# Patch embedding of a small vision tower: token rows 1 and 2 share one product with summed weights, rows in the order 0, 3, 1, 2

## The reference

```python
p = PATCH                                   # 16
shifts = ((1, -1, 1, -1), (-1, 1, -1, 1), (-1, 1, 1, -1), (1, -1, -1, 1))
parts = [x] + [_shift2d(x, HALF * s[2], HALF * s[0]) for s in shifts]
xc = jnp.concatenate(parts, axis=1)         # image and four copies shifted by 8
patches = ...reshape(B, h * w, p * p * C5)  # 16 tokens of 3840 values
mu = patches.mean(axis=-1, keepdims=True)
var = patches.var(axis=-1, keepdims=True)
xn = (patches - mu) * jax.lax.rsqrt(var + LN_EPS) * ln_gamma + ln_beta
return jnp.einsum('bnp,dp->bnd', xn, W) + b # 192 values a token
```

## Time and profile before

| what | us |
|---|---|
| median of 3 runs | 692.64 |
| the profiled execution, its own time | 691.0 |
| its span, first to last instruction | 689.2 |
| PE busy (share of the span) | 506.5 (73%) |
| DVE busy | 354.6 (51%) |
| ACT busy | 163.7 (24%) |
| POOL busy | 156.5 (23%) |
| L680, the patch products: busy | 99.1 |
| first product of `qk(0)` at | 122.4 |

### The profile page before, as it was taken

How to read it: one execution, slowest core, us unless ns; L and a number is a source line. 1 busy time by engine, 2 the same in 40 slices (tenths; PEclk the granted TensorE clock), 3 DMA queues, 4 the chain that set the end, 5 groups by cost and what they waited for, 6 DMA issues and landing times.

```text
span 689.2 us, 13111 instructions
## 1 busy us (share of the span) xinstructions
PE 506.5 (73%) x4632; PEld 450.1 (65%) x4633; DVE 354.6 (51%) x1088; ACT 163.7 (24%) x341; POOL 156.5 (23%) x156
## 2 busy tenths in 40 slices
PE   4999996996314516199999269621899999999960
PEld 4999996456313413189998266401799999999960
DVE  1599995466999885522212567667122212222216
ACT  4100001223793224043332040300221222112210
POOL 2894000000001000224442100001244444444320
PEclk9999998998656558599999789865799999999995
DMA  9960000000004002376659500202666555655516
GB/s 327 412 220 11 1 1 0 2 3 2 1 0 162 1 0 92 81 206 178 176 161 351 179 1 0 92 0 64 186 175 178 174 164 172 179 173 160 139 48 249
DMA packets 35235, 81.41 MB, mean 118 GB/s; under 512 B 6870, under 2 KB 17970, under 8 KB 34034
## 3 DMA queue, kind: packets, MB, share of 16 engines
q1 hardware_dynamic: 29618, 69.36, 30.8%
q0 software_dynamic: 5568, 11.41, 6.3%
HBM read 70.33 MB, written 10.42 MB: 117 GB/s over the span
## 4 chain that ended last, share of the span: by engine, by line
PE 63%; DVE 23%; DMA 5%; ACT 4%; issue 3%; SPq 1%; POOL 0%; ACTq 0%; DVEq 0%; POOLq 0%
PE ps L925 17%; PE ps L680 13%; PE ps L905 11%; PE ps L909 7%; DMA xT<-rows,from_i 2%; DVE stat L1028 2%; PE ps L750 2%; PE ps L751 2%; DVE h L1574 2%; PE ps L778 1%; PE ps L864 1%; DMA arena<-tok_w 1%; DVE xT L1450 1%; PE ps L890 1%; PE ps L655 1%
## 5 line engine op out<-in xcount | busy, mean ns | idle before, releaser
L925 PE MATMUL ps<-arena,xn 128*128 x696 | 128.1, 334 | 0.6 <-ACT xn L596 0.6
L925 PEld LDWEIGHTS ps<-arena,xn 128*128 128x128 f32 x696 | 111.5, 190 | 7.5 <-issue 0.8
L680 PE MATMUL ps<-arena 128*128 128x192 f32 (+1 forms) x672 | 99.1, 334 | 9.1 <-ACT arena L446 8.5
L680 PEld LDWEIGHTS ps<-arena 128*128 128x128 f32 (+1 forms) x672 | 97.4, 195 | 9.8 <-ACT arena L446 8.2
L408 POOL DMA_INDIRECT xT<-rows,from_i x58 | 56.5, 973 | 181.8 <-DVE to_i L1484 164.7
L420 POOL DMA_INDIRECT made<-xT,to_i x58 | 57.2, 987 | 155.5 <-DVE xT L1507 99.9
L905 PE MATMUL ps<-xT,arena 128*128 128x128 f32 x696 | 89.7, 280 | 0.0
L905 PEld LDWEIGHTS ps<-xT,arena 128*128 128x128 f32 x696 | 84.9, 197 | 0.1
L1507 DVE COPY xT<-ps 128x192 f32<-128x192 f32 x39 | 13.9, 357 | 134.1 <-PE ps L925 134.1
L599 ACT ACTIVATE xn<-ps 128x384 f32<-128x384 f32 x78 | 34.0, 488 | 137.2 <-PE ps L910 129.8
L909 PE MATMUL ps<-xT,arena 64*128 64x128 f32 x348 | 54.8, 292 | 0.0
(11 more groups left out here) (339 smaller groups left out, 740.8 us busy)
## 6 DMA issues: line engine op xcount, KB each, us to landing
arena<-ffn_a SPq DMA_DIRECT2D x58, 384.0 KB
arena<-ffn_b SPq DMA_DIRECT2D x116, 96.0 KB
arena<-x_blocks SPq DMA_DIRECT2D x16, 384.0 KB, 7.2
arena<-x_strips SPq DMA_DIRECT2D x3, 1536.0 KB, 12.2
arena<-ffn SPq DMA_DIRECT2D x4, 1152.0 KB, 11.5
rows<-xn SPq DMA_DIRECT2D x8, 384.0 KB, 2.5
xn<-made SPq DMA_DIRECT2D x8, 384.0 KB, 4.2
arena<-tok_w SPq DMA_DIRECT2D x8, 288.0 KB, 7.4
```

Source lines behind the costliest of these rows:

```text
L680: mm = pe.matmul(tok_ps(t), xs[rows, strip % GRID, 2 * j + b, 128 * c:128 * c + 128], wg[rows, w_chunk(P, b) + c, :], start=bank not in op ...
L925: mm = pe.matmul(ps[:, 6 + u, 0:DIM], hT[:, u, 128 * c:128 * c + 128], F["w2"][:, bass.ds(e2 + DIM * c, DIM)], start=(c == 0), stop=(c == ...
```

## The change

It touches the patch embedding up to `qk(0)`. With strips x1, x2, x3 and weights W0, W1 (P = 0, 1), row 1 is x1 W0 + x2 W1 and row 2 is x2 W0 + x3 W1. The change computes m2 = x2 (W0 + W1) once, and adds (x1 - x2) W0 to get row 1 and (x3 - x2) W1 to get row 2. Its parts:

- VectorE forms `w_row` = W0 + W1; GpSimd subtracts strip 2 from strips 1 and 3 in place, when rows 0 and 3 have used them, in two halves each (`x_less`).
- TensorE's order is row 0, row 3, m2, row 1, row 2: 294 products for 336. Row 2 shares banks with row 0, so it waits for row 0's drain. The weight transposes now go to banks 2, 3, 6, 7, and wait for the drain of m2 (`m2_out`).
- `h` is set by ScalarE (scaling, signal `h_scaled`) and GpSimd (addition, `h_set`) instead of VectorE. VectorE drains rows 0 and 3, then m2 into rows 1 and 2, then rows 1 and 2. Two of the four normalisations of a row are ScalarE's.
- `attention_weights` moves from behind the block statistics to before load 4; its weights are loaded earlier, strip 3 before strip 2. `projection_rows` comes before row 0.
- Each row is transposed into banks of its own; ScalarE takes seven of the eight copies, VectorE the last.
- Some semaphores are merged, and their counts moved.

```diff
+TOK_ROWS = (0, 3, 1, 2)
+TURN_BANKS = (2, 6, 4, 0)
+SUM_AT = {"y0": 0, "y3": 6, "m2": 2, "y1": 4, "y2": 0}
...
@@ sync
             blocks_in(0, 4)
+            for tile, part, row, n in QKV_TILES:
+                sp.dma_start(wnat[part:part + n, tile, :], qkv_w[row:row + n, :]).then_inc(sem("wnat_in"), 16)
+            for c in range(2):
+                sp.dma_start(wnat[0:96, 5 + c, :], proj_w[96 * c:96 * c + 96, :]).then_inc(sem("wnat_in"), 16)
+            sp.dma_start(xs[:, 3], x_strips[:, 3]).then_inc(sem("x_in3"), 16)
             sp.dma_start(cst[:], consts).then_inc(sem("cst_in"), 16)
             sp.dma_start(xs[:, 2], x_strips[:, 2]).then_inc(sem("x_in2"), 16)
-            blocks_in(4, 8)
-            sp.dma_start(xs[:, 3], x_strips[:, 3]).then_inc(sem("x_in3"), 16)
-            blocks_in(8, 16)
+            blocks_in(4, 16)
             sp.dma_start(tok_b_row[:], tok_b).then_inc(sem("tok_b_in"), 16)
@@ gpsimd, behind w_sums
+            for n, strip in enumerate((1, 3)):
+                pool.wait_ge(sem("tok_ps"), n + 1)
+                pool.wait_ge(sem("x_in2"), 16)
+                for odd in (1, 0):
+                    pool.tensor_tensor(xs[:, strip, odd::2], xs[:, strip, odd::2], xs[:, 2, odd::2],
+                                       ALU.subtract).then_inc(sem("x_less"), 1)
+            pool.wait_ge(sem("tok_bc_ready"), 1)
+            for n, i in enumerate(TOK_ROWS):
+                pool.wait_ge(sem("h_scaled"), n + 1)
+                four = h[:, 4 * i:4 * i + 4, :]
+                pool.tensor_tensor(four, four, tok_bc[:, 1:2, :].to_broadcast([128, 4, DIM]), ALU.add).then_inc(sem("h_set"), 1)
@@ scalar
+            act.wait_ge(sem("tok_y"), 1)
+            for i in TOK_ROWS:
+                for t in range(4 * i, 4 * i + 4):
+                    ins = act.activation(h[:, t, :], tok_bc[:, 0, :], ACT.Copy, scale=stat[:, 200 + t:201 + t])
+                ins.then_inc(sem("h_scaled"), 1)
...
+                for n, i in enumerate(range(4) if stage else TOK_ROWS):
+                    if stage == 0:
+                        act.wait_ge(sem("near_xn"), n + 1)
+                        if n == 2:
+                            act.wait_ge(sem("wT_ps"), 1)
...
+                    for t in (4 * i + 2, 4 * i + 3):
+                        ins = act.activation(xn[:, t, :], h[:, t, :], ACT.Identity, bias=stat[:, 480 + t:481 + t], scale=stat[:, 464 + t:465 + t])
+                    ins.then_inc(sem("xn_act"), 1)
@@ tensor
+            for n, (name, strip, P) in enumerate((("y0", 1, 1), ("y3", 3, 0), ("m2", 2, 2), ("y1", 1, 0), ("y2", 3, 1))):
+                if n < 3:
+                    pe.wait_ge(sem(f"x_in{strip}"), 16)
+                if name == "m2":
+                    pe.wait_ge(sem("w_row"), 1)
...
+                if name == "y2":
+                    pe.wait_ge(sem("tok_out"), 4)
                 for b in COLS:
+                    if n >= 3 and b in (-1, 0):
+                        pe.wait_ge(sem("x_less"), 2 * (n - 3) + 1 + (b == 0))
@@ vector
+            dve.tensor_tensor(w_row, wg[:, 0:12, :], wg[:, 12:24, :], ALU.add).then_inc(sem("w_row"), 1)
...
             for m in range(16):
+                if m == 4:
+                    dve.wait_ge(sem("wnat_set"), 1)
+                    dve.wait_ge(sem("wnat_in"), 128)
+                    attention_weights()
...
-            for t in range(NTOK):
-                ins = dve.scalar_tensor_tensor(h[:, t, :], tok_bc[:, 0, :], ny[:, t:t + 1], tok_bc[:, 1, :], ALU.mult, ALU.add)
...
+            projection_rows()
+            for n, i in enumerate(TOK_ROWS):
+                if n == 2:
+                    dve.wait_ge(sem("tok_ps"), 3)
+                    for r in (1, 2):
+                        dve.wait_ge(sem("h_set"), r + 2)
+                        for j in range(GRID):
+                            t = 4 * r + j
+                            ins = dve.scalar_tensor_tensor(h[:, t, :], sum_ps("m2", j), y[:, t:t + 1], h[:, t, :], ALU.mult, ALU.add)
+                    ins.then_inc(sem("m2_out"), 1)
```

More of the change, by code:

```diff
@@ L126, in build @@
         gb = view(at, [60]); at += 60
+        w_row = view(at, [12, DIM]); at += 12 * DIM
         assert at <= 33024
@@ L464, in transposed @@
                                    ACT.Copy).then_inc(sem("xT0_ready"), 1)
-            transposed(0)
+            norms(0)
+            for n, i in enumerate(TOK_ROWS):
+                act.wait_ge(sem("xT_ps"), n + 1)
+                for x, rws, off in ((xT0, slice(0, 128), 0), (xT1, slice(0, K1), 1)):
+                    if n == 3 and off:
+                        continue
+                    act.activation(x[rws].rearrange("p (b t) -> p b t", t=NTOK)[:, :, 4 * i:4 * i + 4],
+                                   ps[rws, TURN_BANKS[n] + off, :].rearrange("p (j b) -> p b j", j=4),
+                                   ACT.Copy).then_inc(sem(f"xT{off}_ready"), 1)
             def queries(tb):
@@ L667, in _, with part, w_of @@
             opened, left = set(), {}
-            for P in range(2):
-                for i in range(GRID):
-                    for b in COLS:
-                        for j in range(GRID):
-                            left[4 * i + j] = left.get(4 * i + j, 0) + 3 * (0 <= 2 * j + b < NB)
-            def part(i, j, P, b, c):
-                strip = i + P
-                rows = slice(64, 128) if strip == 0 else slice(0, 64) if strip == GRID else slice(0, 128)
-                t, bank = 4 * i + j, 2 * i + j // 2
-                left[t] -= 1
-                mm = pe.matmul(tok_ps(t), xs[rows, strip % GRID, 2 * j + b, 128 * c:128 * c + 128], wg[rows, w_chunk(P, b) + c, :],
-                               start=bank not in opened, stop=left[t] == 0, skip_group_check=True)
-                opened.add(bank)
-                return mm
+            for name, runs in (("y0", 2), ("y3", 2), ("m2", 1), ("y1", 1), ("y2", 1)):
+                for j in range(GRID):
+                    left[name, j] = 3 * runs * sum(0 <= 2 * j + b < NB for b in COLS)
+            def part(name, j, strip, rows, w, b, c):
+                left[name, j] -= 1
+                mm = pe.matmul(sum_ps(name, j), xs[rows, strip, 2 * j + b, 128 * c:128 * c + 128], w[rows],
+                               start=(name, j // 2) not in opened, stop=left[name, j] == 0, skip_group_check=True)
+                opened.add((name, j // 2))
+                return mm
+            def w_of(P, b, c):
+                return wg[:, w_chunk(P, b) + c, :]
             def columns(b):
@@ L721, in _ @@
                     for c, j in columns(b):
-                        mm = part(i, j, P, b, c)
-                if (i, P) in ((0, 1), (1, 1), (2, 1), (3, 0)):
-                    mm.then_inc(sem("tok_ps"), 1)
+                        w = w_row[:, 3 * (b + 1) + c, :] if P == 2 else w_of(P, b, c)
+                        mm = part(name, j, strip, slice(0, 128), w, b, c)
+                mm.then_inc(sem("tok_ps"), 1)
             pe.wait_ge(sem("wT_ready"), 1)
```

166 lines of the change are left out of this document (83 added, 83 removed).

## The result

The changed kernel takes 696.3 us, the median of 8 runs (695.99 to 699.1), against 691.17 of 8 runs of the kernel before beside it (689.88 to 694.15). The ratio is 1.0067, 95% interval 1.0047 to 1.0086: slower, by little more than what was called measurable. The forecast was 693.3, within 678.0 to 698.5. The profiled execution took 696.26 us, its span is 694.4, and the mean granted clock is 0.85 for 0.866. TensorE is busy for 501.0 us instead of 506.5, VectorE for 368.8 instead of 354.6, GpSimd for 185.0 instead of 156.5.

A forecast was written before the change was run, and what follows sets the result against it. TensorE bounds the stage, then a VectorE tail; after the change VectorE bounds. Start of qk(0) -0.2 plus clock 0.9 gives +0.7 us: 691.7 profiled, 693.3 as median, range 678.0 to 698.5.

The forecast's parts named there:

- the slower rival: Projection rows: their six scalings also wait under GpSimd's four additions, +4.1 us on the sum, 697.4; chance of slower 0.14.
- the sum: Whole forecast: VectorE and GpSimd both wait, VectorE becomes the bound; +0.7 us, median 693.3; chance 0.45.
- step 2: VectorE after w_row: statistics of the first four block loads to 26.1, then two reductions at once, to 29.1.
- Short operations: attention_weights: sixteen short VectorE operations, two passing per GpSimd operation, take 10.5 us instead of 3.0, ending at 39.6.
- variant in which those on 7 elements pass: attention_weights: operations on 7 elements don't wait; same time as only VectorE waiting, 689; chance 0.29 for both together.
- Long ones: attention_weights: seven long VectorE operations, 8.6 us before, each wait out one GpSimd operation, + 8.2; end 56.5.
- GpSimd held: GpSimd's weight sums: 2.4 us late, then held 6.8 us by the seven long VectorE operations, ending at 68.3.
- Only VectorE waits: GpSimd's sums run on as before to 59.1, some 4.3 us off the sum, 689; chance 0.29, shared.
- Projection rows: projection_rows before row 0: 2.9 us; only VectorE's last cast waits for GpSimd's second addition, to 90.3.
- TensorE: Patch products: idle 8.6 us for tok_b_row till 72.4, row 2 from 91.7, end 110.6, before VectorE at 112.3.
- Tail: Row 2's scales to qk(0): two normalisations 0.7, seven copies and start, 117.8 to 122.2 against 122.44, -0.2 us.
- Clock: TensorE idle ahead of qk(0): low clock costs between nothing and 1.75 us, 0.9 taken.

The follow-up runs named there:

- e1: Changed kernel with six of eight steps of GpSimd's weight sums left out and strip subtractions started only after attention_weights; computes something else: 681.19 us, ratio 0.9814.
- e4: Changed kernel with the load of tok_b_row issued ahead of the block loads of m = 4 on: 698.7 us, ratio 1.0077.
- e5: Changed kernel with ScalarE's six copies of the turns of rows 0, 3 and 1 moved before its wait for row 2's scales: 697.86 us, ratio 1.0063.
- e6: Changed kernel with twenty transposes of a constant added on TensorE ahead of the turn of row 2: 694.68 us, ratio 1.0019.
- e3: Changed kernel with projection_rows moved behind the last row's layer norm, away from GpSimd's four additions to h: 693.75 us, ratio 0.9998.
- e10: e7 with ScalarE multiplying the weights by beta in place, and GpSimd waiting for the quantisation before going on: 675.79 us, ratio 0.9752.
- e11: e10 with projection_rows moved behind VectorE's last copy of a turn: 672.63 us, ratio 0.9709.
- e7: Changed kernel with the edits of e3, e4, e5 and e6 together, and the ten weight transposes behind row 2's products: 688.68 us, ratio 0.9945.
- e2: Changed kernel with attention_weights moved back behind the chain of the scales: 704.19 us, ratio 1.0145.
- e8: e10 with the same instructions, but GpSimd adding and subtracting as soon as its inputs are ready, not waiting for the quantisation: 695.81 us, ratio 1.0027.

## Why the prediction was right, and where it was off

The result lies 3.0 us above the forecast and inside its range. The case that it named likeliest, both engines wait and VectorE becomes the bound, is what happened, but the mechanism of the slower rival came on top of it, and that rival's 697.4 is nearer to 696.3 than the sum's 693.3. A kernel slower by over 0.5% had been given a chance of 0.24 in all. By its own steps:

1. *w_row and the first blocks*: forecast to end at 21.9 and 26.1, ended at 21.56 and 25.9. Then VectorE waited until 27.41 for the DMA of `proj_w`. The prediction let step 2 begin at once; it had asked of the moved blocks' loads whether they arrive, but not of the weights' own, which the change puts behind four block loads.
2. *Short operations*: forecast 10.5 us, took 10.4 (30.46 to 40.87). The variant in which those on 7 elements pass falls.
3. *Long ones*: forecast 16.8 us for seven, took 15.6. The end at 56.5 was hit by luck: this and the DMA cancel.
4. *GpSimd held*: forecast sums' end 68.3, was 66.7. "Only VectorE waits" falls with the 3.44 of `w_row`'s neighbour and with 1.64 to 2.90 for the seven beside the long ones.
5. *Blocks* end: 78.4 forecast, 78.6. *Subtractions*: 3.45 each forecast, 13.58 for four. *Scales*: 85.1 forecast, 83.6, the earlier sums passed on.
6. *Projection rows*: **the mis-sized term.** The sum let VectorE be free at 90.3, behind the one cast that waits; it was free at 93.5. Less the 1.5 us by which the chain was early, the step cost 4.7 us more than priced. The argument against it was that they take 0.28 for 128 elements where a cast takes 0.23, and so don't run at a cast's rate. The traces of five kernels (the changed one, e1, e4, e5, e6) show four of the six waiting all the same, with 1.68 to 1.85 us each. e3, which takes them away from there, wins 4.8 us back, so the price that the rival had put on it, 4.1, was about right. Duration per element was a poor witness for what an operation shares.
7. *Rows*: a turn forecast at 6.14 took 6.05, the shared drain 2.69 for 2.78. Row 2's scales: 117.8 forecast, 120.5, the 3.2 us of step 6 less 0.5.
8. *TensorE*: the wait for `tok_b_row` till 72.4 was till 72.97, row 2's start 91.7 was 94.98, the end 110.6 was 114.85. The forecast had it end 1.7 us before VectorE is free for row 2; VectorE was free at 114.50 and waited 0.41 us for it, since the last 18 records of patch products took 4.82 us, at a mean granted clock of 0.64 from 110.0 to 114.8. e5 and e6 have the same idle time before them (2.46) and 3.19 at full clock, so this stretch isn't in every execution. That the products saved on TensorE buy nothing was the main statement; e4 bears it out, as the wait that it saves came back in full.
9. *Tail*: 4.4 us from scales to `qk(0)` forecast, 4.4 measured; ScalarE's two normalisations take 0.98 for 0.7, and the copies pass a little faster.
10. *Clock*: 0.9 taken, 1.75 the upper end, 2.9 measured. **The second mis-sized term, outside its own bounds.** The earlier trace rows had shown one low stretch of 3.5 us, and the bound was made of its length at half rate. The low level lasted from 121.6 into the fourth pair, after 130.

Against its own profiled execution the forecast was +0.7, and +5.3 came: 2.65 by the start of `qk(0)` (step 6, 4.7, less what came early, 1.5, and 0.5 on the way), and 2.0 by the clock. Against the medians it missed by less, 3.0 us, and that is luck: it had added 1.64 us to the profiled 691.0 for a median of 692.64, but beside the changed kernel that median was 691.17, and the changed kernel's profiled execution (696.26) was at its own median.

By the Trainium skill (SBUF — State Buffer, "Who interferes with whom") a VectorE operation with at most one SBUF input outside the two-port modes doesn't contend with GpSimd, while `tensor_scalar` can enter such a mode. By the first half of that the six scalings with pointer scalars, at 0.28 us for 128 elements, looked safe; the 1.7 us show that they aren't. Whether it is such a mode or the pointer scalar that makes them wait, no run here separates.

That the change can gain is shown by e10 and e11. In e10 TensorE's work up to the weight transposes ends at 97.4 where it ended at 110.6 before, close to the 13.7 us of the 42 products, and the ratios are 0.9752 and 0.9709. But these kernels also carry the repairs of e7 and ScalarE's scalings, so the gain isn't that of the changed kernel with one edit.

## What to carry to other kernels

When work comes off the bounding engine, lay the timeline of the next one beside that of every engine that shares something with it, at the new times of a moved block and not at the old ones: the same instructions were worth 20 us more or less by when GpSimd's ran. Operations on one SBUF tensor that reduce or take statistics can stand beside GpSimd's; two-tensor operations, copies and scalings, short linked ones above all, pay for the whole operation that they meet, so give GpSimd long operations only where VectorE has the former. And when a wait of the bounding engine is removed without gain (e4), look for it again further down before looking elsewhere.

## What the hardware showed that was not expected

- Scalings with pointer scalars from one SBUF tensor, 96 x 128, wait for GpSimd (1.68 to 1.85 us where they take 0.28 to 0.34 alone), though their duration is above that of a cast on as many elements a partition (0.23). The drains from PSUM, with one operand in SBUF, don't: four took 1.39 under the additions in e3, as elsewhere.
- The holding is mutual: 1.14 became 3.44 for GpSimd, 0.17 became 3.36 for VectorE. Beside GpSimd operations of 1.15 to 1.41 us every other linked short operation of VectorE waited. Beside the subtractions of 3.4 us that alternation failed: in e2 four in a row waited 3.35 each, in e8 two. Where long operations of both meet, both are stretched (e8: 4.85 for 1.56, and 8.15 for two of 3.43).
- TensorE's granted clock in `qk(0)` differed with small differences in the idle time before it. Where the turn of row 2 had run at full rate, an idle time of 0.82 (e8, e11) or 1.10 us (e7) left the first pair at 1.10 us, and behind one of 1.77 (e10) or 2.20 (e6) it took 1.65 and 1.87. Over the first 3.5 us the granted clock was 1.00 in e7, 0.57 in e10 and 0.53 in e6. A turn at the low level alone doesn't decide: behind one, and an idle time of 0.82 each, the kernel before has 1.10 and e5 2.04.
